# Moving one bin in seven of a graph kernel's message stage: a scaling to ScalarE, a first difference from GpSimd to VectorE

## The reference

```python
for l in range(N_LAYERS):
    f1 = relu(x[row] @ nb_W[l] + nb_b[l])
    f2 = relu(x[col] @ self_W[l] + self_b[l])
    h = relu(concatenate([f1, f2], axis=1) @ att1_W[l] + att1_b[l])
    log_alpha = (h @ att2_W[l] + att2_b[l])[:, 0]
    mask = clip(sigmoid(log_alpha) * (ZETA - GAMMA) + GAMMA, 0.0, 1.0)
    rowsum = segment_sum(mask, row, num_segments=n) + 1e-06
    d_inv_sqrt = clip(rowsum ** (-0.5), 0.0, 10.0)
    vals = mask * d_inv_sqrt[row] * d_inv_sqrt[col]
    x = segment_sum(vals[:, None] * x[col], row, num_segments=n)
    out = out + x
```

## Time and profile before

| | us |
|---|---|
| median of 3 runs | 4171.06 |
| the profiled execution's own time | 4178.5 |
| its span, first to last instruction | 4176.8 |
| TensorE busy | 3757.2 (90%) |
| VectorE busy | 3586.6 (86%) |
| GpSimd busy | 2799.7 (67%) |
| ScalarE busy | 2013.5 (48%) |

### The profile page before, as it was taken

The page is one execution under the profiler, slowest core; times in us unless marked ns, Lnnn a source line. Parts: engine busy times, 40 slices in busy tenths (PEclk is TensorE's granted clock), DMA queues, the critical chain, the costliest instruction groups (busy, mean ns, idle before and its releaser), DMA issues. The chain is left out here.

```text
span 4176.8 us, 261652 instructions
## 1 busy us (share of the span) xinstructions
PE 3757.2 (90%) x99727; PEld 3572.9 (86%) x99728; DVE 3586.6 (86%) x5801; ACT 2013.5 (48%) x5437; POOL 2799.7 (67%) x4756
## 2 busy tenths in 40 slices
PE   5888668888779999899988999999997999989998
PEld 4777568888759999899978999999996999989997
DVE  7999968888768888799987888799996788879998
ACT  4898858888721111466641111156663111136664
POOL 2777533333235666899974666699995566679998
PEclk7888889999979999999999999999998999999999
DMA  1000089999727777566645777666662677756665
GB/s 36 14 15 15 13 263 334 341 341 331 280 93 249 244 241 251 172 182 180 180 114 184 240 246 245 232 161 180 180 180 86 232 250 240 248 183 182 180 180 145
DMA packets 586273, 800.11 MB, mean 192 GB/s; under 512 B 126790, under 2 KB 528154, under 8 KB 586170
## 3 DMA queue, kind: packets, MB, share of 16 engines
q1 hardware_dynamic: 550106, 719.89, 55.3%
q0 software_dynamic: 36064, 78.85, 6.3%
HBM read 672.34 MB, written 126.04 MB: 191 GB/s over the span
## 5 line engine op out<-in xcount | busy, mean ns | idle before, releaser
L1329 PE MATMUL pre_ps<-rows_a,hot_ab 128*128 128x64 bf16 x21609 | 1302.8, 194 | 47.3 <-ACT rows_a L1425 26.3
L1329 PE MATMUL pre_ps<-table,hot_ab 128*128 128x64 bf16 x21609 | 1302.1, 194 | 6.7 <-issue 6.7
L1553 POOL TENSOR_TENSOR message<-message 128x448 f32<-128x448 f32 x1029 | 1302.6, 1303 | 5.4 <-ACT message L1478 4.3
L1329 PEld LDWEIGHTS pre_ps<-rows_a,hot_ab 128*128 128x128 fp8e4 x21609 | 1131.3, 98 | 76.0 <-issue 52.6
L1329 PEld LDWEIGHTS pre_ps<-table,hot_ab 128*128 128x128 fp8e4 x21609 | 1133.7, 98 | 7.2 <-issue 7.2
L1614 DVE TENSOR_TENSOR message<-message 128x448 f32<-128x448 f32 x1029 | 1003.5, 976 | 17.3 <-POOL message L1553 17.3
L1478 ACT ACTIVATE message<-pre_ps,mask 128x64 f32<-128x64 f32 x3087 | 745.3, 312 | 441.3 <-PE pre_ps L1376 416.5
L1602 DVE SCALAR_TENSOR_TENSOR message<-pre_ps,w 128x448 f32<-128x448 f32 x1029 | 642.5, 624 | 288.3 <-PE pre_ps L1329 210.0
L1376 PE MATMUL pre_ps<-table,hot_ab 128*128 128x64 bf16 x21609 | 804.0, 194 | 60.8 <-DVE message L1631 45.9
L1376 PEld LDWEIGHTS pre_ps<-table,hot_ab 128*128 128x128 fp8e4 x21609 | 755.1, 98 | 84.1 <-issue 76.7
L1585 DVE TENSOR_REDUCE logit<-message 128x7 f32<-128x448 f32 x1029 | 626.2, 609 | 0.0
(11 more groups left out here) (177 smaller groups left out, 5088.2 us busy)
## 6 DMA issues: line engine op xcount, KB each, us to landing
hot_ab<-hot_scratch SPq DMA_DIRECT2D x2058, 224.0 KB, 3.9
hot_scratch<-hot SPq DMA_DIRECT2D x343, 336.0 KB, 5.9
both<-hot_scratch SPq DMA_DIRECT2D x147, 784.0 KB, 5.1
places<-slots_scratch POOLq DMA_DIRECT2D x196, 224.0 KB, 6.4
places<-slots_scratch POOLq DMA_DIRECT2D x98, 336.0 KB, 7.3
slots_scratch<-bins SPq DMA_DIRECT2D x392, 16.0 KB, 1.4
out<-res SPq DMA_DIRECT2D x1, 1536.0 KB
raw<-in_src SPq DMA_DIRECT2D x1, 768.0 KB
```

Source lines behind the costliest of these rows:

```text
L1329: last = nc.tensor.matmul(pre_ps[g][:, j, :], hot[:, b, g, end, j * P:(j + 1) * P].bitcast(FP8), table, start=end + part == 0, stop=end == ...
L1553: pool.tensor_tensor(message[:, g, :, 1, :], message[:, g, :, 0, :], top[:, g, :, 0, :, 1], ALU.subtract).then_inc(s["rest_ready"], 1)
```

## The change

`LOW` goes from 4 to 3, so bin 3 of each group is scaled by ScalarE in place of VectorE. A new constant `OWN` = 1 splits the first difference: GpSimd computes it for bins 1 to 6, VectorE for bin 0. VectorE's new instruction, `first_of_own`, is written at the end of each group, behind third. It waits for VectorE's own low scaling, and third waits for it as well (`own_ready`).

```diff
-    LOW = min(4, G - 1)
+    LOW = min(3, G - 1)
+    OWN = 1
...
-                    pool.tensor_tensor(message[:, g, :, 1, :], message[:, g, :, 0, :], top[:, g, :, 0, :, 1],
+                    pool.tensor_tensor(message[:, g, OWN:G, 1, :], message[:, g, OWN:G, 0, :], top[:, g, OWN:G, 0, :, 1],
                                        ALU.subtract).then_inc(s["rest_ready"], 1)
...
+                def first_of_own(q, r, g, b):
+                    dve.wait_ge(s["low_scaled"], q + 4)
+                    dve.tensor_tensor(message[:, g, 0:OWN, 1, :], message[:, g, 0:OWN, 0, :], top[:, g, 0:OWN, 0, :, 1],
+                                      ALU.subtract).then_inc(s["own_ready"], 1)
+
                 def third(q, r, g, b):
+                    dve.wait_ge(s["own_ready"], q + 1)
                     dve.wait_ge(s["rest_ready"], q + 1)
...
                         late(r, g, b, 2, first, third)
+                        first_of_own(q, r, g, b)
```

More of the change, by code:

```diff
@@ L1262, in masks_and_messages @@
                        "inverted first_ready left_ready second_ready row_ready pool_step tail_step "
-                       "fetched low_scaled high_scaled rest_ready third_ready added total_taken row_done "
+                       "fetched low_scaled high_scaled rest_ready own_ready third_ready added total_taken row_done "
                        + sems, again=True) as (s, block):
```

## The result

The changed kernel takes 4499.91 us (median of 4 runs, 4498.4 to 4500.51), beside 4171.61 for the kernel before (4 runs, 4166.67 to 4175.13): 1.0796 times as long, 95% interval 1.0783 to 1.0808. The profile's span is 4498.7 us.

The account below looks back on a forecast made before the run. It took the bound to be the alternating turns of GpSimd's sub and VectorE's third; 294 us for the chain plus 38 for take_total, 332 in all, gave 4503 us against 4171.06, range 4405 to 4680.

Parts of the forecast that it names:

- The bound is neither engine but their turns: Message stage: GpSimd's sub and VectorE's third alternate, one turn each per group, which sets the pace of 1.274 us.
- A waiting sub is let in between two VectorE operations that follow without a gap: Message stage: GpSimd's sub goes ahead of first_of_own, right behind third; read from L379 in the sort stage.
- the nearest rival (4191): Message stage: VectorE keeps the turn through third and first_of_own, low scaling stays hidden; about +20 us, 4191; chance 0.09.
- L366's row: Sort stage: a GpSimd instruction of 4.74 us, held past L543 and L546 as well; stands against sub being let in.
- The chain and its size: Message stage: low scaling, third, sub, first_of_own in sequence; 1.56 us a group against 1.274, 294 us over 1029.
- take_total: VectorE, message stage: hidden before, now in the chain; 0.26 us in about 144 rows, 38 us.
- The moved scaling is free, and sub gives up 0.11: Message stage: ScalarE's fourth scaling instruction costs nothing; GpSimd's sub, 64 elements fewer, gets 0.11 us shorter.
- the rival of the kept turn: Message stage: VectorE holds its turn through third and first_of_own; 1.29 us a group, 4191 us; chance 0.09.
- TensorE's clock was left at full: TensorE, message stage: full clock assumed though only 77% busy; no profile row shows the clock at 77%.
- The rule that the small piece pays its start-up: VectorE's first_of_own: fixed cost of some 151 cycles per instruction, 0.22 us for 64 elements; the sum is not moved.

Follow-up runs that it names:

- OWN = 2: Changed kernel with two bins in place of one in VectorE's share of the first difference (128 elements, 320 for GpSimd): 4455.43 us, ratio 1.0687.

## Why the prediction was right, point by point

*The bound is neither engine but their turns.* Shown from both sides. VectorE relieved of 0.07 us a group: no change. VectorE given 0.14 us more with one input: no change. One element with two inputs: 440 us. The turn taken away again, by reading from PSUM: 66 us less than the kernel before.

*A waiting sub is let in between two VectorE operations that follow without a gap.* This was the step on which the forecast and the nearest rival (4191) parted, and it was read from an earlier stage on 36 elements. It held: first_of_own, begun at 3012.92, stood right behind third, and sub ended first. Its median by source in the changed kernel is 0.84 us, so it is not the odd case:

```profile
L1615 DVE TENSOR_TENSOR message<-message x1029: 209/843/847, 1703.4 to 4479.9; 128x64 f32<-128x64 f32 x172
```

L366's row stays unexplained. There is one more like it in the kernel before (the first line, past one VectorE operation), and the changed kernel's trace has the long one again (the second line), so it is no accident of one run:

```profile
54.45 2.25 POOL L366 TENSOR_TENSOR local<-key,bases 128x36 bf16 x1 [7.93 <-DVE twin L535]
...
64.21 4.74 POOL L366 TENSOR_TENSOR local<-key,bases 128x36 bf16 x1 [2.90 <-DVE twin L535]
```

In the message stage first_of_own was held as forecast; why L366 is not let in is open.

*The chain and its size.* Predicted 1.56 us a group, measured 1.57. Third's end was put at 0.87 after low scaling's start (3013.00 - 3012.12 = 0.88), sub's at 1.55 (1.57), first_of_own's at 1.63 (1.64).

*take_total.* Predicted 0.26, measured 1.78 - 1.57 = 0.21 to 0.22, since there sub goes ahead of third and the chain is another one: 0.42 us to sub's start, 0.83 for sub, 0.47 to third's end, 0.14 to first_of_own's, less the overlap of 0.08. The two errors cancel: 885 groups with 1.566 - 1.274 = 0.292 and 144 with 1.789 - 1.274 = 0.515 are 258 + 74 = 332 us, the same as the 332 of the prediction, and the measured difference is 4499.91 - 4171.61 = 328. That the forecast of 4503 lay within 4 us is therefore in part luck; that it lay near is not.

*The moved scaling is free, and sub gives up 0.11.* Both held: 4171.48 for the one; for the other sub ends 0.69 behind third where 448 elements took 0.79, and a further bin of it was worth 44 us (0.11 less 0.07, times 1029, is 41).

*Details that were off.* First_of_own was expected to be about 0.75 us long; it is 0.84, because it begins before third ends. GpSimd was put at about 1.2 of 1.56 us busy; it has 204.99 us in 189 groups, 1.08 each. TensorE was put at 77% busy; the window has 254.66 of 300, 85%. The 1.20 us of the prediction counts fetch and add_up as they overlap in the record (0.77 + 0.76 less the overlaps), and where a fetch now has to wait, one of the overlaps is gone (add_up ends and the next fetch begins at 3014.18). In the rival of the kept turn a sum is slightly off: 1.274 - 0.11 + 0.12 is 1.284, not 1.29, so about +10 us and 4181 in place of 4191, which changes nothing in the choice.

TensorE's clock was left at full: the window's mean is 0.97 of 2.4 GHz, so it fell to 1.2 GHz for short stretches, for example in this one:

```profile
3001.20:3004.60 3.40, 3.17 (x46) 3.09 (x47) 3.40 (x8) 1.22 (x6) 2.38 (x3) 0.50 0.27 67
```

It cost nothing here: low scaling begins at 3000.94, 3002.50 and 3004.07, 1.56 and 1.57 us apart, the same pace as at full clock.

*The rule that the small piece pays its start-up.* The prediction cited the VectorE page of the Trainium skill (VectorE: DVE Perf Modes, The TRN2 errata) for 0.22 us; the free first_of_own takes 0.21. That fits and is beside the point: 0.14 us of VectorE's time was free here, as the one-input instruction shows.

The Trainium skill's SBUF — State Buffer (SBUF: two separate sides) says that VectorE and GpSimd share one pair of SBUF ports, that a VectorE instruction with two SBUF inputs or a GpSimd one, whichever starts first, gets the pair for its whole length, and that the other is fully blocked. The held durations shown here, 0.84, 0.88, 1.20 and 1.25 us, agree: in each case the sub had begun before the instruction that was held. L366's two rows do not. That the elements of a held instruction pass in what is left after the other's end (0.07 us of first_of_own's 0.84) is this trace's own.

The advice of the Trainium skill's GPSIMD Engine Reference (Engine selection), elementwise work to VectorE, holds here per element (OWN = 2 is faster than OWN = 1) and fails per instruction.

## What to carry to other kernels

When VectorE and GpSimd are both busy all the time, compare the shortest and the median duration of the same instruction. If both engines' are stretched, as here (0.61 and 1.02, 0.93 and 1.31), suspect that they hold each other; what counts is then how many times per round they take turns, more than how much each does. Before you add a VectorE instruction beside a busy GpSimd, count its SBUF tensor inputs. Here one was free where two cost the wait for a whole GpSimd instruction, and pulled what had been hidden under it (low scaling, third) into a chain. Where one of the two inputs could come from PSUM, the turn disappeared.

## What the runs showed that I had not expected

- A mask column in SBUF, used as the per-partition factor beside a PSUM input and one SBUF tensor, does not make an instruction of the kind that is held: 268 to 284 ns in all 1029 (the expectation had left this open):

```profile
L1616 DVE SCALAR_TENSOR_TENSOR message<-pre_ps,mask,message x1029: 268/271/284, 1696.0 to 4079.4; 128x64 f32<-128x64 f32 x172
```

  It is longer, though, than the 0.21 us of the plain difference of the same 64 elements, and than the 0.2 I had put.
- The order of two VectorE instructions alone was worth 105 us (4499.91 to 4604.55), with no engine's work changed. The prediction had nothing on the order; the expectation of that run, written once the result was known, had it at 4600.
